# Swapping the key projection with the second row maximum, and the output addition with the first, in a two-layer attention kernel

## The reference, cut to what matters

```python
xn  = layernorm(x)                                  # 4 x 1024 x 128
qkv = (xn @ W_qkv).reshape(b, s, 16, 64, 3)         # 16 heads of 64
scores  = einsum('bqhd,bkhd->bhqk', q, k) / 8
weights = softmax(scores, axis=-1)
attn = einsum('bhqk,bkhd->bqhd', weights, v)
s = attn.reshape(b, s, 1024) @ W_out                # 1024 -> 128
x = x + s * silu(mixture_of_experts(xn))
```

## Time and profile before

| | |
|---|---|
| median of three runs | 1810.33 us (1805.15 to 1813.97) |
| profiled execution, its own time | 1797.12 us |
| its span | 1795.3 us |
| granted TensorE clock, mean | 0.983 |
| busy: TensorE matmul / VectorE / ScalarE / GpSimd | 95% / 79% / 81% / 80% |

### The profile page before, as it was taken

How to read it: one execution, slowest core, us unless ns; L and a number is a source line. 1 busy time by engine, 2 the same in 40 slices (tenths; PEclk the granted TensorE clock), 3 DMA queues, 4 the chain that set the end, 5 groups by cost and what they waited for, 6 DMA issues and landing times. The chain is left out here.

```text
span 1795.3 us, 32822 instructions
## 1 busy us (share of the span) xinstructions
PE 1698.5 (95%) x9247; PEld 927.9 (52%) x9247; DVE 1421.9 (79%) x2053; ACT 1446.5 (81%) x1954; POOL 1442.1 (80%) x871
## 2 busy tenths in 40 slices
PE   5899999999999999999999999999999899985687
PEld 5445444444444454444444444544444688862456
DVE  7877777777777777777777777777777898888896
ACT  4488888888888888888888888888888688864643
POOL 4399889999899998899998999998999266745573
PEclk9899999999999999999999999999999999997899
DMA  7213131312223131313132231213131787331001
GB/s 261 74 61 97 47 96 50 105 51 94 72 71 106 59 97 47 96 55 99 53 94 73 71 106 59 97 47 96 54 103 49 249 250 245 100 108 38 6 13 30
DMA packets 155030, 160.63 MB, mean 89 GB/s; under 512 B 48241, under 2 KB 128177, under 8 KB 151794
## 3 DMA queue, kind: packets, MB, share of 16 engines
q1 hardware_dynamic: 150002, 149.93, 27.2%
q0 software_dynamic: 4992, 10.27, 1.7%
HBM read 103.98 MB, written 27.90 MB: 73 GB/s over the span
## 5 line engine op out<-in xcount | busy, mean ns | idle before, releaser
L1609 POOL TENSOR_TENSOR psum_k<-psum_k,probs 128x1024 f32<-128x1024 f32 x384 | 925.8, 2411 | 78.9 <-ACT probs L1544 53.8
L1544 ACT ACTIVATE probs<-ps_s 128x1024 f32<-128x1024 f32 x512 | 496.6, 1022 | 136.8 <-PE ps_s L1362 136.2
L1371 PE MATMUL ps_v<-probs,V 128*64 128x512 f32 x2056 | 498.4, 605 | 0.0
L1628 DVE TENSOR_REDUCE mxh<-ps_three 128x2 f32<-128x1024 f32 x264 | 321.6, 1218 | 73.8 <-PE ps_three L1329 70.2
L1371 PEld LDWEIGHTS ps_v<-probs,V 128*64 128x64 f32 x2056 | 125.1, 136 | 232.8 <-issue 196.2
L1528 ACT ACTIVATE ps_s<-qkv_raw 128x1024 f32<-128x1024 f32 x224 | 243.9, 1129 | 0.0
L1528 ACT ACTIVATE ps_s<-peak 128x1024 f32<-128x1024 f32 x224 | 243.3, 1127 | 0.0
L1362 PE MATMUL ps_s<-e_ew 64*128 64x512 f32 x1536 | 199.4, 391 | 0.0
L1650 DVE TENSOR_REDUCE mxh<-ps_three 128x2 f32<-128x1024 f32 x128 | 156.7, 1224 | 43.1 <-PE ps_three L1329 43.1
L1609 POOL TENSOR_TENSOR psum_k<-probs 128x1024 f32<-128x1024 f32 x64 | 152.6, 2384 | 32.5 <-ACT probs L1544 24.4
L1362 PEld LDWEIGHTS ps_s<-e_ew 64*128 64x128 f32 x1536 | 146.1, 185 | 27.1
(11 more groups left out here) (323 smaller groups left out, 3197.6 us busy)
## 6 DMA issues: line engine op xcount, KB each, us to landing
e_ew<-w_split SPq DMA_DIRECT2D x23, 1024.0 KB
qkv_raw<-peaks SPq DMA_DIRECT2D x33, 512.0 KB, 3.8
V<-e_x_raw SPq DMA_DIRECT2D x33, 512.0 KB, 3.6
peak<-peaks SPq DMA_DIRECT2D x32, 512.0 KB, 3.7
e_y_row<-shares SPq DMA_DIRECT2D x128, 128.0 KB, 2.9
xs_hi<-xh SPq DMA_DIRECT2D x16, 512.0 KB, 4.0
xs_lo<-xl SPq DMA_DIRECT2D x16, 512.0 KB, 5.1
rows<-in_blank_d SPq DMA_DIRECT2D x4, 1483.5 KB, 16.2
```

The source lines that it names most:

```text
L1371: ins = nc.tensor.matmul(ps_v[rows, :], V[par][:, kt, rows], probs[:, t % RING, x, :], start=kt == 0, stop=kt == KT - 1)
L1544: nc.scalar.activation(probs[:, t % RING, :, :], ps_s[t % 2][:, :, :], ACT.Exp, scale=SCALE).then_inc(p_done, 1)
L1609: nc.gpsimd.tensor_tensor(acc, probs[:, (t - 1) % RING, :, :] if kt == 1 else acc, probs[:, t % RING, :, :], ALU.add).then_inc(add_done, 1)
L1628: nc.vector.tensor_reduce(mxh[:, kh, t, :], max_bank(unit, i)[:, :, :], AX.X, ALU.max).then_inc(m_done, 1)
```

## The change

```diff
--- TensorE, odd step of a visit
                     scores(n, par, t)
                     if p in SHARED:
                         row_max_shared(n, t, i, other, unit % 2)
-                    elif VISIT[p][0][0] == "K":
-                        item(n, par, VISIT[p][0], b)
-                        row_max(n * 2 + unit, i, other, unit % 2)
                     else:
                         row_max(n * 2 + unit, i, other, unit % 2)
                         item(n, par, VISIT[p][0], b)
--- VectorE, half()
                     row_max_shared(n, t + 3)
+                    step(t + 4)
                     add_out(n, f"out{1 - hf}")
-                    step(t + 4)
                     inverse(n, hf)
                     step(t + 5)
                     low(n, late, par)
```

## The result

The changed kernel takes 1837.43 us (median of six runs, 1829.87 to 1841.49), the kernel before 1810.47 (six runs). The ratio is 1.0132 with a 95% interval of 1.0108 to 1.0156: 27 us slower. The forecast was 1839 us.

A forecast was written before the change was run, and what follows sets the result against it. The prediction read the attention as bound by TensorE, its added waits lost in full. 0.31 + 0.60 = 0.91 us per pass, over 32 passes 29.1 us, added to the 1810.3 us median gave 1839 us, range 1820 to 1850.

The forecast's parts named there:

- The order costs nothing by itself, only a wait can: TensorE, maximum and key projection: either order puts values 3.15 to 3.16 us behind the first maximum; only waits move time.
- First reduction: VectorE: it waits for its products and mx_done, starting 0.60 us behind the first maximum, bounds 0.55 and 0.63.
- Second maximum: TensorE: it waits for the first reduction to end and starts 1.88 us behind the first maximum.
- Addition: VectorE's output addition: starts 1.14 us after the reduction's start, register work hidden under it, and ends at 2.43.
- Key projection behind the addition: TensorE: the projection follows the addition's end by 0.14 us with K1 and 0.43 with K0, starting at 2.57 and 2.86.
- the rival in which the sequencer keeps its lead: TensorE's register work is done ahead of the wait; projection 0.06 us behind the addition, 1821.8 us in all; chance 0.14.
- `values`: TensorE: they follow the projection by 0.89 us, so start 0.31 us later with K1 and 0.60 with K0.
- What else moves: Other engines: VectorE gains slack, the inverse comes about 0.3 us later without loss, the seeds stay hidden.
- The seeds stayed hidden: ScalarE's seeds for the next visit's second scores arrive 0.07 us early; rival that they become the bound: about 1849, chance 0.11.
- The chain of the inverse: inverse and its two DMAs move 0.3 us later; the normalisation waiting for them loses nothing.
- the reductions of L1628 to wait for their products in 64 cases more: Sign in the profile after: VectorE's L1628 waits for TensorE's L1329 in 64 more cases.
- Sum: 0.31 + 0.60 = 0.91 us per pass, 29.1 us over 32 passes; low ends 22.4 us, high ends 35.2.

The follow-up runs named there:

- experiment 7: Changed kernel, with TensorE forming the next visit's first maximum ahead of the output projection: 1.0069 of the kernel before, a pass 41.53 us.
- experiment 10: Kernel before, with the first maximum moved ahead of the output projection and zeros filled in place of the expert-weight subtraction: 1.0084, a pass 41.75 us.
- experiment 3: Changed kernel, with staged-weight waits ahead of the wait for the addition and key projections reading tokens at a fixed place: 1.0051 of the kernel before.
- experiment 4: Changed kernel, with the two waits for staged weights added in the visits with K1 too: 1.0115 of the kernel before.
- experiment 5: Changed kernel, with K0's staged-weight waits moved ahead of the wait for the addition, the address staying behind it: 1.0091 of the kernel before.
- experiment 2: Kernel before, with only VectorE's order changed (first reduction ahead of the output addition), TensorE as before: 1.0454, a pass 43.90 us.
- experiment 6: Kernel before, with both edits (TensorE's and VectorE's) in the visits with K1 alone: 1.0026, a pass 41.32 us.
- experiment 11: Kernel before, with a fill of zeros in place of the expert-weight subtraction: 1.0016, a pass 41.04 us.

## Why the prediction was right

By its own steps:

- *The order costs nothing by itself, only a wait can.* Right. Where the wait is covered (experiment 7) the order of the change is even the faster one: with the same early maximum and nobody held by the port, a pass takes 41.53 in that order and 41.75 in the old one (experiment 10).
- *First reduction.* Taken at 0.60, measured 0.55. The wait on `mx_done` behind the wait for the products cost nothing; I had given it 0.05.
- *Second maximum.* 1.88 forecast, 1.83 measured, the same 0.05.
- *Addition.* 1.14 behind the reduction and its register work hidden under it: right, 633.23 to 634.37.
- *Key projection behind the addition.* 0.14 and 0.43 forecast, 0.15 and 0.44 measured. This is the term that separates the forecast from the rival in which the sequencer keeps its lead, and experiments 3 to 5 take it apart: 0.06 with nothing behind the wait, 0.2 for the staged weights of `K0`, the rest (0.18 and 0.09) for the address.
- *`values`.* +0.31 and +0.60 forecast, +0.26 and +0.55 measured; only the 0.05 is off.
- *What else moves.* The seeds stayed hidden; TensorE's weight loads wait for them in 64 cases, 10.6 us in all, without a later start. The chain of the inverse cost nothing that these runs show. I expected the reductions of L1628 to wait for their products in 64 cases more; they do so in 54 more (75 before, 129 now at L1625). I wrote that VectorE only gains slack; in truth the subtraction now starts before one of GpSimd's additions has ended (it takes 0.58 instead of 0.41), and experiment 2 shows how near 1.10 us more were. I hadn't named that neighbour.
- *Sum.* 0.91 us per pass forecast, 0.81 in the visits, 0.74 in the pass. The last 0.07 lie in the half behind `K1`, in the visit with `Q1`: from `values` to the denominators and from there to the next maximum it took 1.80 and 1.00 in the kernel before, 1.77 and 0.96 in the changed one. It is gone in experiments 6 and 11 too. The sum had put this visit at no change, and it was a gain.

The traces show where that gain comes from. VectorE's L1683 multiplies two SBUF tensors, and like the subtraction it ends 0.28 behind the addition that GpSimd has under way, in both kernels (before: GpSimd 631.95, L1683 632.24). GpSimd, then the kernel before:

```profile
627.03 4.92 POOL L1609 TENSOR_TENSOR psum_k<-psum_k,probs 128x1024 f32<-128x1024 f32 x2
```
```profile
633.30 0.68 DVE L1663 TENSOR_TENSOR e_ew<-ps_three,e_ew 128x512 fp32r<-128x512 f32 x1
```
```profile
634.10 1.08 PE L1309 MATMUL ps_three<-psum_k,ones 128*64 128x512 f32 x4
```

`low` of the queries (L1663), two instructions behind L1683, frees the bank of the denominators. It ends at 633.98, and TensorE starts them 0.12 behind that, with one register operation of the sequencer (L1307) in between: they were held. In the changed kernel L1683's counterpart starts later against GpSimd and takes 1.19 instead of 1.42, `low` ends 0.32 ahead of the denominators, and they are not held:

```profile
640.47 4.94 POOL L1606 TENSOR_TENSOR psum_k<-psum_k,probs 128x1024 f32<-128x1024 f32 x2 [0.21 <-ACT probs L1541]
```
```profile
644.50 1.19 DVE L1680 TENSOR_TENSOR e_y_row<-e_y_row 128x256 f32<-128x256 f32 x1
```

Medians over the loop say the same: L1683 takes 1.41 and `low` ends 0.13 ahead of the denominators before, 1.19 and 0.32 in the changed kernel.

The forecast was 29 us; the passes give 23.7, the medians 27, with an interval of 20 to 28. By the passes the same base would give 1834 and not 1839.

## What to carry to other kernels

A wait costs more than the wait: when an engine's sequencer loses its lead, the address and register work that stands behind the wait comes on top, here 0.1 us with one instruction and 0.4 with three. Put satisfied waits and arithmetic ahead of the one wait that will be late, and before exchanging two steps ask which engine had been early for whom. Idle time on an engine off the path (90 us here) is cover for someone else's wait; and a short instruction that shares a port with a long one on another engine can stand on an edge, here 0.41 us in the kernel before and 2.11 us in experiment 2, where it starts 0.56 behind the start of GpSimd's addition.

## What the runs showed of the hardware

- A matmul whose wait hangs on itself starts 0.06 us behind its releaser (experiment 3). With one register instruction of 56 ns between, 0.15 (the changed kernel, `K1`); with one of 148 ns, 0.24 (experiment 5); with three sequencer instructions, 0.44 (the changed kernel, `K0`).
- Two waits that are met cost 0.2 us behind the late wait and nothing ahead of it (experiments 4 and 5), and the trace, not the kernel's text, tells on which side they stand.
- Between two matmul groups, start to start, TensorE takes longer where the tiling changes: 0.24 from scores to a maximum of the same tiling (experiment 7), 0.34 from scores to a full-array projection, 0.43 from a maximum to the output projection (experiment 7).
- A subtraction of 128x256 that takes 0.41 us took 2.11 and 2.63 beside GpSimd's additions of 2.4 us, and a fill of the same size in the same place 0.27. The held instruction ends 0.28 us behind GpSimd's.
